# Layer-1 weights of a two-layer attention kernel: split early, parked in DRAM and transferred back

## The reference, cut to what matters

```python
xn = layernorm(x, g_in)                  # g_in is folded into the weights
q  = xn @ Wq                             # 512 x 1024
k, v = split(xn @ Wkv)                   # 512 x 128
p  = softmax(q k' + bias, causal, masked)
x  = x + layernorm((p @ v) @ Wo) * g_out # Wo: 1024 x 512
```

## Time and profile before

| | us |
|---|---|
| median of 3 runs | 1342.87 (1341.12 to 1344.15) |
| the profiled execution | 1338.76 |
| its span, first to last instruction | 1337.0 |
| mean granted PE clock | 0.988 of full |

### The profile page before, as it was taken

One profiled execution on the slowest core, in us unless ns is written; L12 is line 12 of the kernel. 1 busy time (PEld: TensorE's weight loads), 2 busy tenths in 40 slices (PEclk: granted clock), 3 DMA queues, 4 the chain that ended last, 5 costly groups with the idle time before them and its releaser, 6 DMA issues.

```text
span 1337.0 us, 28861 instructions
## 1 busy us (share of the span) xinstructions
PE 1284.9 (96%) x8152; PEld 1184.9 (89%) x8152; DVE 1105.9 (83%) x2968; ACT 860.0 (64%) x3246; POOL 752.9 (56%) x1340
## 2 busy tenths in 40 slices
PE   3798999999999999999899999999999999999997
PEld 3687999999999999999798999999999999999996
DVE  5677777787777777778889999899899999999985
ACT  3565666766666666666766666766666666666663
POOL 6443444444444444444366766776776766776673
PEclk8799999999999999999999999999999999999999
DMA  9013401111110110111421101101111110110111
GB/s 288 33 33 52 82 24 47 47 35 35 47 47 24 47 47 24 47 47 35 131 99 37 48 25 47 47 27 44 47 34 37 47 45 26 47 47 24 47 32 41
DMA packets 44007, 67.51 MB, mean 50 GB/s; under 512 B 7408, under 2 KB 15632, under 8 KB 43968
## 3 DMA queue, kind: packets, MB, share of 16 engines
q1 hardware_dynamic: 42752, 66.89, 16.4%
q0 software_dynamic: 384, 0.12, 0.1%
q10 hardware_dynamic: 832, 0.04, 0.0%
HBM read 48.16 MB, written 18.87 MB: 50 GB/s over the span
## 4 chain that ended last, share of the span: by engine, by line
PE 89%; DVE 5%; issue 2%; ACT 1%; POOL 1%; SPq 1%; DMA 1%; POOLq 0%; DVEq 0%; ACTq 0%
PE bank_q L1202 29%; PE bank_y L1334 25%; PE bank_s L1202 12%; PE bank_o L1202 10%; PE bank_p L1301 6%; PE bank_t L1274 4%; PE bank_t L1242 2%; DVE wo_l L858 1%; PE bank_t L1279 1%; DMA x_in<-in_x 1%; DVE wq_l L849 0%; DVE wq_raw L886 0%; ACT p_raw L719 0%; DVE pt_l L1069 0%; DVE qt_l L1001 0%
## 5 line engine op out<-in xcount | busy, mean ns | idle before, releaser
L719 ACT ACTIVATE p_raw<-s_sb,neg_m 128x130 f32<-128x130 f32 (+1 forms) x1024 | 372.0, 367 | 144.6 <-DVE neg_m L1059 142.8
L564 POOL TENSOR_TENSOR p_sb<-p_raw,rden 128x256 f32<-128x256 f32 x256 | 157.6, 616 | 356.7 <-DVE rden L1065 356.5
L1202 PE MATMUL bank_q<-wq_h,xt_h 128*128 128x384 f32 x768 | 269.3, 351 | 7.3 <-DVE xt_l L957 7.1
L1202 PE MATMUL bank_q<-wq_h,xt_l 128*128 128x384 f32 x768 | 261.1, 340 | 0.0
L1202 PE MATMUL bank_q<-wq_l,xt_h 128*128 128x384 f32 x768 | 260.6, 339 | 0.0
L554 POOL TENSOR_TENSOR bias_g<-bias,mask_row 128x260 f32<-128x260 f32 x256 | 177.6, 694 | 124.2 <-DVE s_sb L1052 122.5
L1334 PE MATMUL bank_y<-wo_h,ot_h 128*128 128x512 f32 x512 | 219.1, 428 | 0.3 <-DVE ot_l L1075 0.3
L1334 PE MATMUL bank_y<-wo_h,ot_l 128*128 128x512 f32 x512 | 203.1, 397 | 0.0
L1334 PE MATMUL bank_y<-wo_l,ot_h 128*128 128x512 f32 x512 | 202.8, 396 | 0.0
L719 ACT ACTIVATION_READ_ACCUMULATOR p_raw<-s_sb,neg_m 128x1 f32 x1024 | 193.3, 189 | 0.0
L1052 DVE TENSOR_TENSOR s_sb<-bank_s,bias_g 128x392 f32<-128x392 f32 x256 | 142.9, 558 | 37.5 <-PE bank_s L1202 37.5
(11 more groups left out here) (127 smaller groups left out, 3107.4 us busy)
## 6 DMA issues: line engine op xcount, KB each, us to landing
x_in<-in_x SPq DMA_DIRECT2D x32, 256.0 KB, 2.8
x_res<-in_x SPq DMA_DIRECT2D x32, 256.0 KB, 2.6
x_mid<-y_out SPq DMA_DIRECT2D x32, 256.0 KB, 2.0
x_in<-x_mid SPq DMA_DIRECT2D x32, 256.0 KB, 2.8
x_res<-x_mid SPq DMA_DIRECT2D x32, 256.0 KB, 2.7
out_x<-y_out SPq DMA_DIRECT2D x32, 256.0 KB, 2.0
wq_raw<-in_L_cond_Wq SPq DMA_DIRECT2D x4, 768.0 KB, 6.6
wo_raw<-in_L_cond_Wo SPq DMA_DIRECT2D x1, 2048.0 KB, 12.9
```

Of the source, the lines that this page charges most:

```text
L564: e.tensor_tensor(to[:, 0:2 * P].rearrange("p (e j) -> p e j", e=2), low_blocks(of)[:, :, 2:LOW], r[:, 0:2, :].broadcast_to([P, 2, P]), AL ...
L719: last = e.activation(p_raw[:, g % 2, lo:hi], s_sb[:, g % 2, lo:hi], ACT.Exp, bias=neg_m[:, h:h + 1], accum_out=esum[:, h:h + 1])
L1202: last = e.matmul(out, a, b, start=(k == 0), stop=(k == len(passes) - 1))
```

## The change

1. Layer 1's raw weights are loaded earlier: `load_wq(1)` in step 16 and `load_wo(1)` in step 17.
2. In each of steps 18 to 27 one batch is split: 2 of the 4 row blocks of one part of Wq (6 batches, 128x384 each), or 2 of the 8 row blocks of Wo (4 batches, 128x512 each). ACT writes the two high pieces into the former `w1_sb` (`high_parts`, ahead of the first exponentials of the step). POOL makes the two low pieces in place in the raw tile (`low_part`, one after `normalise` 0 and one after `normalise` 2): a multiplication by g_in and a subtraction for Wq, a subtraction alone for Wo.
3. SP stores each batch to DRAM in the step after, as two transfers (`store_batch`), ahead of the store of x.
4. In step 30 POOL issues six transfers that bring the pieces of Wq back (part 0 after `normalise` 0, parts 1 and 2 after `normalise` 2), each once PE has finished that part of layer 0. In step 32 it issues four for Wo (half 0 ahead of `normalise` 3, half 1 behind it). PE waits for them before item (1, 0).
5. All weight work for layer 1 leaves the steps 30 and 32 on ACT and DVE.
6. The loop of layer 0 ends at item 15, so steps 16 to 35 are unrolled.

```diff
@@ -34,7 +34,12 @@
 EPS = 1e-5
 TINY = 1e-24
 BIG = 1e38
-FIRST, LAST = 4, B - 4
+FIRST, LAST = 4, (15, B - 4)
+RAW_Q, RAW_O, SPLIT = 16, 17, 18
+BATCHES = [("q", p, 2 * k) for p in range(3) for k in range(2)] + [("o", 0, 2 * k) for k in range(4)]
...
@@ -114,9 +119,9 @@
     straight(0, FIRST)
     for layer in range(LAYERS):
-        with e.Fori(FIRST, LAST + 1) as i:
+        with e.Fori(FIRST, LAST[layer] + 1) as i:
             step(lambda d: (layer, i + d))
-        straight(layer * B + LAST + 1, (layer + 1) * B + FIRST if layer + 1 < LAYERS else N + 2)
+        straight(layer * B + LAST[layer] + 1, (layer + 1) * B + FIRST if layer + 1 < LAYERS else N + 2)
 def build(nc, x, bias0, cond, mask0, mask1, g_in, null_bias, wq, wkv, wo, g_out, q_scale, k_scale,
...
@@ -125,6 +130,8 @@
     x_mid = nc.dram_tensor("x_mid", (B, P, D), F32, kind="Internal").ap()
     table = nc.dram_tensor("bias_table", (H, P, 2 * P), F32, kind="Internal").ap()
+    wq_store = nc.dram_tensor("wq_store", (2, P, len(PARTS), KC, 6 * DH), F32, kind="Internal").ap()
+    wo_store = nc.dram_tensor("wo_store", (2, P, OC, D), F32, kind="Internal").ap()
     x_of = [x, x_mid]
     out_of = [x_mid, out]
...
@@ -212,6 +219,7 @@
         y_t, x_out = y_out[:, 0, :], y_out[:, 1, :]
         w1_sb = sb("w1_sb", [P, KC, D])
+        high = w1_sb[:, :, :].rearrange("p c n -> p (c n)").rearrange("p (b k n) -> p b k n", b=2, k=2)
         w2_sb = sb("w2_sb", [P, KC, H])
         b2_col = sb("b2_col", [H, 1])
         pos_i = sb("pos_i", [P, 1], I32)
...
@@ -317,6 +331,19 @@
          MM1, PRE2, ST2, MV2, VE2, RSTD2, CEN2, GAIN2, EXP2, PLUS2, REC2, SILU2, TP2, TCOPY2,
          MM2, TABLE) = range(1, 31)
+        def pieces(j):
+            kind, p, c0 = BATCHES[j]
+            if kind == "q":
+                lo, hi = part_columns(p)
+                return [(c, wq_raw[:, c, lo:hi], high[:, j % 2, k, 0:hi - lo]) for k, c in enumerate((c0, c0 + 1))]
+            return [(c, wo_raw[:, c, :], high[:, j % 2, k, :]) for k, c in enumerate((c0, c0 + 1))]
+        def batch_of(m):
+            j = m[1] - SPLIT if isinstance(m[1], int) and m[0] == 0 else -1
+            return j if 0 <= j < len(BATCHES) else None
         block = ctx.enter_context(nc.Block())
...
@@ -384,6 +411,8 @@
                     if m[0] == 1:
                         e.wait_ge(x_stored, (m[1] + 1) * 16)
                     load_x(m)
+                if (m := at(-1)) is not None:
+                    store_batch(m)
                 if (m := at(0)) is not None:
                     bulk(m)
                 if (m := at(-1)) is not None:
...
@@ -395,15 +424,33 @@
                 if is_item(m, 0, 3):
                     e.wait_ge(net_step, TABLE)
                     e.dma_start(table, table_sb.unsqueeze(1).broadcast_to([H, P, 2 * P])).then_inc(table_stored, 16)
-                if is_item(m, 0, B - 3):
+                if is_item(m, 0, RAW_Q):
                     load_wq(1)
+                if is_item(m, 0, RAW_O):
+                    for half in range(2):
+                        e.wait_ge(wo_ready[half], 1)
+                    load_wo(1)
                 if is_item(m, 0, B - 2):
                     e.wait_ge(table_stored, 16)
                     load_bias1()
-                if is_item(m, 0, B - 1):
-                    for half in range(2):
-                        e.wait_ge(wo_ready[half], 1)
-                    load_wo(1)
+            def store_batch(m):
+                j = batch_of(m)
+                if j is None:
+                    return
+                kind, p, c0 = BATCHES[j]
+                cs = slice(c0, c0 + 2)
+                e.wait_ge(low_ready, 2 * j + 2)
+                if j:
+                    e.wait_ge(batch_stored, 32 * j)
+                if kind == "q":
+                    lo, hi = part_columns(p)
+                    to, of = wq_store[:, :, p, cs, :], (high[:, j % 2, :, 0:hi - lo], wq_raw[:, cs, lo:hi])
+                else:
+                    to, of = wo_store[:, :, cs, :], (high[:, j % 2, :, :], wo_raw[:, cs, :])
+                for k in range(2):
+                    e.dma_start(to[k], of[k]).then_inc(batch_stored, 16)
             load_x((0, 0))
             load_wq(0)
...
@@ -534,6 +581,36 @@
                 if is_item(m, 0, 0):
                     output_weights(0, 1)
+            def low_part(m, k):
+                j = batch_of(m)
+                if j is None:
+                    return
+                kind, p, _ = BATCHES[j]
+                c, raw, hi = pieces(j)[k]
+                e.wait_ge(high_ready, 2 * j + k + 1)
+                if kind == "q":
+                    e.wait_ge(g_in_loaded[1], 16)
+                    e.tensor_scalar(raw, raw, g_in_sb[:, 1, c:c + 1], None, ALU.mult).then_inc(raw_scaled, 1)
+                    e.wait_ge(raw_scaled, 2 * j + k + 1)
+                e.tensor_tensor(raw.bitcast(F32R), raw, hi, ALU.subtract).then_inc(low_ready, 1)
+            def bring_back(m, which, half):
+                if not is_item(m, 0, B - 1):
+                    return
+                e.wait_ge(batch_stored, 32 * len(BATCHES))
+                if which == "q":
+                    lo, hi = part_columns(half)
+                    e.wait_ge(q_psum[half], B)
+                    for k, to in enumerate((wq_h, wq_l)):
+                        e.dma_start(to[:, :, lo:hi], wq_store[k, :, half, :, :]).then_inc(wq_back[half], 16)
+                else:
+                    cs = slice(4 * half, 4 * half + 4)
+                    e.wait_ge(wo_half[half], B)
+                    for k, to in enumerate((wo_h, wo_l)):
+                        e.dma_start(to[:, cs, :], wo_store[k, :, cs, :]).then_inc(wo_back[half], 16)
             def between(n):
                 if n == 1:
                     net_deviation(VE2)
...
@@ -594,13 +671,20 @@
                 on(0, masked_bias, 3)
                 on(0, normalise, 0)
+                on(0, low_part, 0)
+                on(1, bring_back, "q", 0)
                 on(1, norms, 0)
                 on(1, norms, 1)
                 on(0, normalise, 1)
                 on(1, norms, 2)
                 on(0, normalise, 2)
+                on(0, low_part, 1)
+                on(1, bring_back, "q", 1)
+                on(1, bring_back, "q", 2)
+                on(-1, bring_back, "o", 0)
                 on(0, start_output)
                 on(0, normalise, 3)
+                on(-1, bring_back, "o", 1)
                 on(1, masked_bias, 1)
                 on(1, masked_bias, 0)
                 inverse_deviations(at)
...
@@ -739,33 +819,29 @@
...
+                on(0, high_parts)
                 on(0, exps, 0)
                 on(0, start_output, 0)
                 on(1, q_out, 0)
...
+            def high_parts(m):
+                j = batch_of(m)
+                if j is None:
+                    return
+                kind, p, _ = BATCHES[j]
+                if kind == "q":
+                    e.wait_ge(wq_loaded[p], 16 * WQ_LOADS[p] * 2)
+                    e.wait_ge(g_in_loaded[1], 16)
+                else:
+                    e.wait_ge(wo_loaded, 16 * 2)
+                if j == 0:
+                    e.wait_ge(net_step, MM1)
+                if j > 1:
+                    e.wait_ge(batch_stored, 32 * (j - 1))
+                for c, raw, hi in pieces(j):
+                    scale = g_in_sb[:, 1, c:c + 1] if kind == "q" else 1.0
+                    e.activation(hi.bitcast(F32R), raw, ACT.Copy, scale=scale).then_inc(high_ready, 1)
             first = (0, 0)
             project_weights(0, 0)
...
@@ -1245,8 +1313,10 @@
             def project(m, p):
                 lo, hi = part_columns(p)
-                if opens_layer(m):
-                    e.wait_ge(wq_ready[p], m[0] + 1)
+                if is_item(m, 0, 0):
+                    e.wait_ge(wq_ready[p], 1)
+                if is_item(m, 1, 0):
+                    e.wait_ge(wq_back[p], 32)
                 if p == 0:
                     wait(e, xt_ready, m)
                     wait(e, q_done[2], m, -1)
...
@@ -1321,8 +1391,10 @@
             def output(m, c0, c1):
-                if opens_layer(m) and c0 % 4 == 0:
-                    e.wait_ge(wo_ready[c0 // 4], m[0] + 1)
+                if is_item(m, 0, 0) and c0 % 4 == 0:
+                    e.wait_ge(wo_ready[c0 // 4], 1)
+                if is_item(m, 1, 0) and c0 % 4 == 0:
+                    e.wait_ge(wo_back[c0 // 4], 32)
                 if is_item(m, 0, 0) and c0 == 0:
                     e.wait_ge(net_step, PRE2)
                 if c0 == 0:
```

More of the change, by code:

```diff
@@ L264, in build @@
         net_step = sem("net_step")
+        high_ready = sem("high_ready")
+        raw_scaled = sem("raw_scaled")
+        low_ready = sem("low_ready")
+        batch_stored = sem("batch_stored")
+        wq_back = sems("wq_back", 3)
+        wo_back = sems("wo_back", 2)
         x_loaded = sem("x_loaded")
@@ L652, in project_weights @@
```

(21 more changed lines are left out.)

## The result

| | before | after |
|---|---|---|
| median, us | 1342.87 | 1334.16 |
| lowest to highest of 5 | 1341.12 to 1346.25 | 1331.06 to 1335.88 |
| the profiled execution, us | 1338.76 | 1334.16 |
| its span, us | 1337.0 | 1332.4 |

The ratio is 0.9932, with a 95% interval of 0.9915 to 0.995: faster by 8.7 us at the medians, where 8.8 was forecast (1334.1). The interval stands for a gain of 6.7 to 11.4 us, so the agreement to 0.1 us is luck.

The account below looks back on a forecast made before the run. PE, busy 96% of the span, was taken as the bound, so gains come only where it waits. The terms -9.37 + 0.5 + 0.1 gave -8.8 us, a median of about 1334.1; the range reached from a gain of 10.4 up to 1339.5.

Parts of the forecast that it names:

- 9.37 - 0.1 us: Steps 30 to 33: 9.37 us of weight work removed, less 0.1 us lost to POOL's issuing in step 32.
- The 5.55 us for step 30: Step 30's share of the 9.37 us that weight work costs at the layer boundary.
- The splitting: Steps 18 to 27: ACT's 1.06 us and POOL's 1.9 us per `low_part` fit idle times, cost nothing.
- Unrolling: 13 more steps of straight code at 0.04 us each, taken as a loss of 0.5 us.
- POOL as issuer: Steps 30 and 32: ten transfers at 0.78 us per issue fit POOL's idle times, except 0.1 us lost.
- The tight end: Step 32, half 1 of Wo: issuing after PE's output just meets DVE's need of the second `masked_bias`; 0.1 us lost.
- The stores: SP's queue: two stores of 786,432 or 1,048,576 B per step, lasting 4.0 to 5.4 us, cost nothing.
- The arrival: Return to layer 1: at 390 GB/s Wq is there at 670.1, in time by 2.4 us; Wo also in time.
- Two signs of being right: At the boundary: POOL's transfers landing in under 7 us each, and no wait of PE for a transfer.
- The slow return: Rival: POOL's casting transfers run slowly, first wait below 288 GB/s, 1354 us at 165 GB/s; chance 0.12.
- The partial return: Rival: transfers at 208 to 288 GB/s, 1336.6 us at 250, or POOL held longer per issue; chance 0.12.
- The costly splitting: Rival: DVE behind POOL's reads loses 0.3 to 0.5 us in each of ten steps, 1337 to 1339; chance 0.10.

Follow-up runs that it names:

- the pair of edits: Changed kernel with layer 1's null key written early and the bias transfers issued in step 28; ratio 0.9938 to the kernel before, step 31 at 19.85 us.
- the control: The changed kernel measured again, with nothing altered; ratio 0.9925 to the kernel before, steps 30 to 33 at 79.82 us.
- the last run: Changed kernel with null key and bias transfers early and SP instead of POOL issuing the return; ratio 0.9922 to the kernel before.
- experiment 4: Changed kernel with three more 0.786 MB transfers on POOL's queue, between the two pieces of each Wq part; ratio 0.9993 to the kernel before.
- experiment 3: Changed kernel with both low pieces of a batch moved behind `normalise` 3, ahead of two `masked_bias`; ratio 0.9982 to the kernel before.

## Why the prediction was right

**Where the time was.** Steps 30 to 33 were to fall by 9.37 - 0.1 us to 79.97; they took 80.03 and 79.82. The run without weights shows that this is what weight work cost: 89.24 - 79.75 = 9.49. The null key as cause is shown for 0.64 of step 31's 0.80 by the pair of edits. Two readings were loose. The high pieces of Wq and the low pieces of Wo stood in the chain, but what PE waited for was DVE's `pt_l`, `qt_l` and `xt_l`. And a change doesn't gain "only where PE waits": 2.0 of the 9.2 us were longer busy time of PE in step 30, where the clock was at 0.93. The 5.55 us for step 30 held both, since they were taken from the length of the step.

**How much was luck.** In the profiles from step 4 to 62 the gain is 8.46 and 8.78 us, which bears out the sum of 8.8. The median's agreement doesn't: the profiled execution was to take 1330.0 and took 1334.16, and the control's gain was 10.1 us.

**The splitting.** Two readings of the kernel after, ACT ahead of the first exponential and POOL behind `normalise` 0, both in step 18:

```profile
414.06 1.13 ACT L878 ACTIVATE w_sb<-wq_raw,g_in_sb 128x384 fp32r<-128x384 f32 x2
416.32 0.41 ACT L799 ACTIVATE p_raw<-s_sb,neg_m 128x130 f32<-128x130 f32 x1 [1.13 <-DVE neg_m L1142]
```

```profile
419.13 1.26 POOL L594 TENSOR_SCALAR wq_raw<-wq_raw,g_in_sb 128x384 f32<-128x384 f32 x1
420.48 1.01 POOL L596 TENSOR_TENSOR wq_raw<-wq_raw,w_sb 128x384 fp32r<-128x384 f32 x1
423.14 0.62 POOL L641 TENSOR_TENSOR p_sb<-p_raw,rden 128x256 f32<-128x256 f32 x1 [1.64 <-DVE rden L1148]
```

ACT's two take 1.13 us (1.06 forecast) and leave 1.13 of the 2.14 idle. POOL's multiplication takes 1.26 us and not the 0.93 that I had set as its upper bound: an operation with one input fewer was not cheaper but dearer. The subtraction takes 1.01. A `low_part` is 2.3 us instead of 1.9 and leaves 1.64 us of the idle time of 3.97. It wasn't stretched by the factor 1.7 that I had allowed for: the twelve multiplications took 1.25 to 1.26 us each. DVE's busy time in such a step is 15.90 us instead of 15.32, and 15.32 again in step 18 of the run that moves POOL's pieces out of it. So DVE is slowed beside them, by 0.6 us a step, where I had 0.5 beside each of two. The Trainium skill, "SBUF — State Buffer", section "Who interferes with whom", has DVE and GpSimd contend for a shared pair of ports; the trace agrees that there is a price, and the step time shows that PE doesn't pay it.

**Unrolling.** 0.04 us a step was right: 19.71 in every unrolled layer-0 step and in the run that only unrolls. Its source was poorer than that: 0.08 of the 0.12 us lay in step 28 alone, the last of the loop (19.75). That excess doesn't multiply, it moves with the end of the loop to step 15 (19.77), and 0.04 is right because the 0.12 was divided by three.

**POOL as issuer.** The timeline of POOL in steps 30 and 32 of the kernel after, which ends in step 33:

```profile
655.61 0.85 POOL L607 DMA_DIRECT2D wq_h<-wq_store  x1
656.46 0.76 POOL L607 DMA_DIRECT2D wq_l<-wq_store  x1
659.63 0.61 POOL L641 TENSOR_TENSOR p_sb<-p_raw,rden 128x256 f32<-128x256 f32 x1 [2.40 <-DVE rden L1148]
...
663.74 0.76 POOL L607 DMA_DIRECT2D wq_l<-wq_store  x1
666.67 0.61 POOL L641 TENSOR_TENSOR p_sb<-p_raw,rden 128x256 f32<-128x256 f32 x1 [2.17 <-DVE rden L1148]
...
708.75 0.58 POOL L612 DMA_DIRECT2D wo_h<-wo_store  x1 [1.03 <-PE bank_y L1406]
...
710.95 0.69 POOL L631 TENSOR_TENSOR bias_g<-bias,mask_row 128x260 f32<-128x260 f32 x1
```

An issue costs 0.75 to 0.85 us for Wq (0.78 forecast) and 0.54 to 0.64 for Wo. `normalise` 1 and 3 still wait for DVE behind them, 2.40 and 2.17 us. The tight end was as tight as forecast. Half 1 of Wo waited for PE's output until 708.75, 18.8 us into step 32 where I had 18.2; its two issues were shorter; and the second `masked_bias` began at 710.95, 21.0 us into the step where I had 20.9. DVE's first scores of step 33 follow it:

```profile
712.13 0.57 DVE L1135 TENSOR_TENSOR s_sb<-bank_s,bias_g 128x392 f32<-128x392 f32 x1 [0.15 <-issue]
```

They begin 2.44 us into the step. In the last run, with SP as issuer, it is 2.20. So DVE is held for 0.2 us, but PE isn't: the step takes 19.75.

**The stores.** I had two stores of 786,432 B a step and 4.0 to 5.4 us for them. Each is half of that, 384 KB (512 KB for Wo), and the medians from issue to landing are 3.9 to 4.9 us. The conclusion, no cost, stands.

**The arrival.** This is the term that was mis-sized. I gave the return 2.4 us of slack; it had none. Two signs of being right failed with it: Wq's six transfers landed in 5.6 to 14.5 us and not in under 7 each, and PE waited for one of them. The row of PE's waits for it (view of waits, 620 to 745 us), then the DMA view of 645 to 725 us in fortieths (2 us each) with Wq's rows:

```profile
PEld bank_q L1270 <- DMA wq_l<-wq_store: 0.2, 1, 0.2
```

```profile
GB/s 0 0 0 0 0 12 217 312 391 369 218 312 302 304 322 367 36 133 189 83 0 0 0 0 0 8 0 62 290 45 74 332 430 422 430 401 20 106 282 5
...
wq_h<-wq_store POOLq DMA_DIRECT2D x3, 768.0 KB, 8.5
wq_l<-wq_store POOLq DMA_DIRECT2D x3, 768.0 KB, 11.1
```

The last piece was to land 670.1 - 643.89 = 26.2 us into step 30; it landed at 663.74 + 14.5 = 678.2, which is 28.8 into it, 0.2 after PE wanted it (669.13 + 8.98 = 678.1). The runs say where the 2.6 us lie. With the bias loads out of the way it landed 24.2 us into the step. So the bias cost the return 4.6 us, a little less than the 5.2 that I gave it, and without it the rate was the 371 to 400 GB/s that I took. But parts 1 and 2 alone, issued from 12.1 us on as I had it (12.9), were to be there 21.0 us into the step and came 3.2 later. I had charged them as if part 0 were gone (its low piece landed only at 15.2), as if the 0.79 MB of x that SP moves in this step were nothing (an estimate at 390 GB/s: 2.0 us), and without the 2 us for landing that I gave to Wo. How the 3.2 us divide among these isn't shown. In all the last piece was 0.2 us late in the profiled execution, and the prediction was right by a narrow margin; experiment 4 shows what 2.4 MB more would have done.

**The rivals.** The slow return did not come about: pieces weren't late by several us. Its threshold, no waiting above 288 GB/s, was wrong, since PE did wait 0.2 us while most slices were at 300 GB/s or more; it was worked out with the same missing terms. The partial return was the nearest rival, and only its first 0.2 us came. The costly splitting appears only when it is moved (experiment 3). Unrolling as a gain of its own is excluded.

## What to carry to other kernels

Work at a change of stage that stands on every engine's path can be spread over earlier steps if each piece fits in a named idle time of the engine that does it; find that idle time in the timeline, since the same piece cost nothing ahead of `normalise` and 1.2 us a step behind it. What then decides is when the results come back: add all that shares the engines between the first release and the first use, the other queues' transfers too, and move whatever can go earlier out of that interval. Bytes alone don't price it: 0.79 MB of bias in rows of 512 and 256 bytes held the return up by 4.6 us, where 0.79 MB at the return's own rate would be 2.0 (an estimate). A stall of PE costs more than its length when the clock falls with it, here 1.5 us on top of 6.0, and busy time alone doesn't show what a change took.

## What the runs showed of the hardware

- A multiplication by a per-partition scalar on POOL (one tensor input, 128x384) takes 1.25 us on the mean of 12, a subtraction of two tensors of the same size 1.02 (the kernel after).
- Transfers on POOL's queue into float32r tiles and on SP's queue into float32 views of them moved the same pieces at the same rate, 371 to 400 and 373 to 387 GB/s in the full slices, with no bias loads beside them.
- Bias loads of 0.79 MB in rows of 512 and 256 bytes on SP's queue made the last of POOL's transfers land 14.5 us after its issue instead of 9.9; without them beside it the slices were at 371 to 400 GB/s, with them at 302 to 322 in the middle.
- With 2.4 MB more on POOL's queue, the x load that SP issued in step 30 landed in 8.1 us instead of 6.3, and DVE waited 2.2 us for it instead of 0.4.
- In step 30 of the kernel before and of the one that is only unrolled, PE's waits were the same (3.2 and 0.2 us), but its clock was 0.93 on the mean in one and 0.87 in the other, and its busy time 1.0 us apart.
- Between 108 and 133 us the granted clock was 1.00 on the mean in four of thirteen profiled executions and 0.80 to 0.86 in nine, whatever the kernel; step 3 then takes 21.09 to 22.58 us instead of 19.64. The changed kernel's two profiled executions differ by 2.8 us, of which 2.5 lie ahead of step 4.
